# Cross attention: values stationary in four column tiles with turned probabilities moving, transposed output evicted and turned back, projections reordered

## The reference, cut to what matters

```python
q = _split_heads(query @ Wq + bq, B, S)
k = _split_heads(key @ Wk + bk, B, key.shape[1])
v = _split_heads(value @ Wv + bv, B, value.shape[1])
scores = jnp.einsum('bhqd,bhkd->bhqk', q, k) / jnp.sqrt(jnp.asarray(D_K, q.dtype))
p_attn = jax.nn.softmax(scores, axis=-1)
x = jnp.einsum('bhqk,bhkd->bhqd', p_attn, v)
x = x.transpose(0, 2, 1, 3).reshape(B, S, H * D_K)
return x @ Wo + bo
...
x = _layernorm(x + _L0_xattn_ref(x, ctx_1024, ctx_1024, ...), axis=-1)
```

## Time and profile before

| what | us |
|---|---|
| median of three executions | 1355.9 |
| the profiled execution | 1359.26 |
| its span in the profile | 1357.5 |
| cross attention, first `make_whole` to the last stored row | 358 to 636 |

### The profile page before, as it was taken

One profiled execution on the slowest core, in us unless ns is written; L12 is line 12 of the kernel. 1 busy time (PEld: TensorE's weight loads), 2 busy tenths in 40 slices (PEclk: granted clock), 3 DMA queues, 4 the chain that ended last, 5 costly groups with the idle time before them and its releaser, 6 DMA issues.

```text
span 1357.5 us, 25935 instructions
## 1 busy us (share of the span) xinstructions
PE 1031.1 (76%) x7366; PEld 774.2 (57%) x7367; DVE 1040.2 (77%) x2363; ACT 767.6 (57%) x1882; POOL 646.2 (48%) x869
## 2 busy tenths in 40 slices
PE   0236786654688888886788888885599999999980
PEld 0234343333566666664466666663588888888870
DVE  6893999997788888873788888873577777777765
ACT  4784643440688888883355555552166666666650
POOL 3895887774355555552244454442423232333324
PEclk9566888877688888886799999997699999999995
DMA  5944000003133333322012222222011111111105
GB/s 192 365 186 194 4 0 31 15 15 117 36 106 105 105 105 105 105 71 62 31 42 82 81 81 81 81 74 75 19 32 38 39 35 39 39 39 39 35 27 188
DMA packets 51884, 105.70 MB, mean 78 GB/s; under 512 B 9808, under 2 KB 36432, under 8 KB 51328
## 3 DMA queue, kind: packets, MB, share of 16 engines
q1 hardware_dynamic: 47472, 92.39, 19.7%
q0 software_dynamic: 4368, 12.78, 3.0%
HBM read 73.06 MB, written 32.10 MB: 77 GB/s over the span
## 4 chain that ended last, share of the span: by engine, by line
PE 35%; DVE 23%; ACT 13%; issue 11%; POOL 8%; DMA 2%; DVEq 0%; POOLq 0%; ACTq 0%; SPq 0%
PE banks L1965 14%; PE banks L1975 10%; POOL whole_level L1104 5%; ACT whole_level L1026 4%; DVE mix_sums L648 3%; ACT att_probs L1464 3%; PE banks L1363 2%; DVE carry L638 2%; DVE carry L635 2%; ACT whole_t L1042 1%; DVE kvq L1635 1%; PE banks L1376 1%; ACT whole L1035 1%; PE banks L1332 1%; DVE q_sin L1602 1%
## 5 line engine op out<-in xcount | busy, mean ns | idle before, releaser
L2048 DVE SCALAR_TENSOR_TENSOR expert_gate<-banks,expert_steps,expert_chunk 128x128 f32<-128x128 f32 x546 | 166.2, 346 | 96.6 <-ACT expert_chunk L2010 94.7
L1965 PE MATMUL banks<-expert_parts,levels 128*128 128x128 bf16 x3276 | 229.2, 220 | 8.1 <-issue 5.5
L1965 PEld LDWEIGHTS banks<-expert_parts,levels 128*128 x3276 | 203.0, 99 | 48.9 <-issue 21.2
L1975 PE MATMUL banks<-down,up 128*128 x546 | 176.2, 406 | 0.0
L2010 ACT COPY expert_chunk<-banks 128x256 f32<-128x256 f32 x273 | 101.7, 373 | 103.6 <-PE banks L1965 103.6
L2103 POOL DMA_INDIRECT chosen_d<-expert_y,expert_target x39 | 38.9, 998 | 204.0 <-ACT expert_y L2020 204.0
L1104 POOL TENSOR_SCALAR whole_level<-whole_level,whole_stat 128x128 f32<-128x128 f32 x112 | 89.3, 808 | 87.6 <-ACT whole_level L1026 87.6
L496 PE MATMUL banks<-x_turned,w_rkv 128*128 128x512 f32 (+1 forms) x192 | 100.5, 683 | 39.0 <-DVE weight L629 38.3
L2014 ACT ACTIVATE silu<-expert_gate,expert_steps 128x128 f32<-128x128 f32 x273 | 110.6, 405 | 15.9 <-DVE expert_gate L2048 15.7
L391 PE MATMUL banks<-consts,level 128*128 128x128 f32 x154 | 35.5, 423 | 87.3 <-POOL level L374 87.3
L2055 DVE SCALAR_TENSOR_TENSOR up<-expert_gate,expert_steps,silu 128x128 f32<-128x128 f32 x273 | 94.6, 346 | 9.3 <-ACT silu L2014 9.3
(11 more groups left out here) (240 smaller groups left out, 2597.6 us busy)
## 6 DMA issues: line engine op xcount, KB each, us to landing
whole_raw<-in_weight_jobs SPq DMA_DIRECT2D x16, 896.0 KB, 5.0
raw<-in_weight_jobs SPq DMA_DIRECT2D x11, 896.0 KB, 5.4
numbers_d<-turned SPq DMA_DIRECT2D x11, 896.0 KB, 5.0
levels_d<-whole_t SPq DMA_DIRECT2D x16, 448.0 KB, 2.7
levels<-levels_d SPq DMA_DIRECT2D x16, 448.0 KB, 3.6
down<-numbers_d SPq DMA_DIRECT2D x16, 448.0 KB, 4.4
finish_moe<-chosen_d SPq DMA_DIRECT2D x8, 512.0 KB, 7.6
normed_d<-normed_parts SPq DMA_DIRECT2D x16, 192.0 KB, 1.9
```

What stands on the lines that cost most here:

```text
L1965: last = pe.matmul(banks[:, at, (m * DC + c) * ROWS:(m * DC + c + 1) * ROWS], levels[:, bass.ds(expert * (2 * JOB) + (m * JOB + (f * DC + ...
L1975: last = pe.matmul(banks[:, Y + j, 0:D], up[j][:, f, :], down[:, bass.ds(expert * JOB + f * D, D)], start=(f == 0), stop=(f == FC - 1))
L2048: last = dve.scalar_tensor_tensor(out=gate[slot(j, f)][:, m, :], in0=halves(at)[:, m, 1, :], scalar=steps[j][:, m, 1, f:f + 1], in1=chunk[ ...
```

## The change: what it does

`sums` exchanges its operands. `v_ones` of a head, widened from 17 to 32 columns (16 values, a one, 15 zeros), is now stationary, and `probs_t` of the head moves, 128 columns. The output of a head is transposed (32 rows by 128 queries); four heads stand below each other in four column tiles (partitions 0, 32, 64, 96), in the second half of bank V. ACT copies the 128x256 of a half to `outs` (`take_outs`), PE turns it back with two 128x128 transposes (`turn_outs`) into HEADS, now 32 columns a head, and DVE's `normalise` reads it there.

The orders change with it. `front` gives up the v projection, which becomes `front_v`, called after `turn_heads`. On PE the output projection `join` goes from before `front` to behind `turn_outs(0, n)`, ahead of scores(0, n+1). On ACT `back` goes from the head of the step to behind `take_qk`. On DVE `normalise(n)` at the end becomes `normalise(n-1)` behind `peaks(1, n)`, and `join(n-1)` goes from before `take_values` to behind `steps_of`. SP and POOL are as before.

The new orders of one step n:

- PE: scores(1, n), turn_outs(1, n-1), turn_probs(0, n), front(n+1), turn_heads(n-1), front_v(n+1), tiles(0), sums(0, n), tiles(1), turn_probs(1, n), turn_outs(0, n), join(n-1), scores(0, n+1), tiles(2), sums(1, n), tiles(3).
- ACT: take_outs(1, n-1), collect(0, n), soften(1, n), take_x(n+1), make_whole(n), round_part 0, take_qk(n+1), back(n-1), tiles(0), round_part 1, take_outs(0, n), tiles(1), collect(1, n), tiles(2), round_part 2, tiles(3), soften(0, n+1).
- DVE: clip(n), peaks(1, n), normalise(n-1), take_values(n+1), steps_of(n+2), join(n-1), peaks(0, n+1).

```diff
 XH, XK = 16, 16
 HALF, QUAD = 8, 4
 BAND = QUAD * XK
+WIDE = 32
 QH, KVH, HD = 8, 2, 128
 REP = QH // KVH
 E, FFN = 8, 896
...
         q_t = [k.buffer(own, f"q_t{j}", [DC, S]) for j in range(2)]
         k_t = [k.buffer(own, f"k_t{j}", [DC, S]) for j in range(2)]
         spread = [k.buffer(own, f"spread{h}", [QUAD, S]) for h in range(2)]
-        v_ones = [k.buffer(own, f"v_ones{j}", [XH, XK + 1]) for j in range(2)]
+        v_ones = [k.buffer(own, f"v_ones{j}", [XH, WIDE]) for j in range(2)]
         x_bias = [k.buffer(own, f"x_bias{j}", [D]) for j in range(2)]
         peak = [k.buffer(own, f"peak{h}", [HALF]) for h in range(2)]
         probs = [k.buffer(own, f"probs{h}", [HALF, S]) for h in range(2)]
         probs_t = [k.buffer(own, f"probs_t{h}", [HALF, S]) for h in range(2)]
+        outs = [k.buffer(own, f"outs{h}", [2, S]) for h in range(2)]
         total = k.buffer(own, "total", [XH])
         heads = [k.buffer(own, f"heads{j}", [XH, XK]) for j in range(2)]
         heads_t = [k.buffer(own, f"heads_t{j}", [DC, S]) for j in range(2)]
...
     exp_ready = k.semaphore("exp_ready")
     probs_turned = k.semaphore("probs_turned")
     probs_t_ready = k.semaphore("probs_t_ready")
+    outs_summed = k.semaphore("outs_summed")
+    outs_ready = k.semaphore("outs_ready")
     heads_summed = k.semaphore("heads_summed")
     heads_ready = k.semaphore("heads_ready")
     heads_turned = k.semaphore("heads_turned")
...
         def front(j, n, i, begin=False):
 
             pe.wait_ge(rows_in[j], 32 * i + 32)
-            if not begin:
-                pe.wait_ge(heads_t_ready, n)
+            if not (isinstance(n, int) and n < 2):
+                pe.wait_ge(whole_read, ROUNDS * (n - 1))
             for c in range(DC):
                 last = pe.transpose(banks[:, TURN, c * P:(c + 1) * P], x_in[j][:, c * P:(c + 1) * P], k.ident)
             last.then_inc(x_turned, 1)
...
                     last = pe.matmul(banks[:, QK, m * P:(m + 1) * P], wq[:, c, m * P:(m + 1) * P],
                                      x_t[j][:, c, :], start=(c == 0), stop=(c == DC - 1))
             last.then_inc(qk_ready, 1)
-            if not begin:
+
+        def front_v(j, n):
+            if not (isinstance(n, int) and n == 0):
                 pe.wait_ge(v_read, n)
-                pe.wait_ge(joined_read, n)
+                pe.wait_ge(outs_ready, 2 * n - 1)
+            if not (isinstance(n, int) and n < 2):
+                pe.wait_ge(joined_read, n - 1)
             for c in range(DC):
                 last = pe.matmul(banks[:, V, 0:D], ctx_t[j][:, c, :], wv[:, c, :], start=(c == 0), stop=(c == DC - 1))
             last.then_inc(v_ready, 1)
...
                     last = pe.transpose(banks[:, PROBS_T + m, a * P:(a + 1) * P], probs[h][:, 4 * m + a, :], k.ident)
                 last.then_inc(probs_turned, 1)
 
-        def sums(j, h, n):
+        def sums(j, h, n, more):
 
             if h == 0:
-                pe.wait_ge(v_read, n + 1)
-                pe.wait_ge(heads_ready, n + 1)
+                pe.wait_ge(v_read, n + 1 + more)
+            else:
+                pe.wait_ge(joined_read, n + 1)
+            pe.wait_ge(outs_ready, 2 * n + h + 1)
             for m in range(2):
                 pe.wait_ge(probs_t_ready, 4 * n + 2 * h + m + 3)
                 for a in range(4):
                     head = HALF * h + 4 * m + a
-                    last = pe.matmul(banks[:, HEADS, head * (XK + 1):(head + 1) * (XK + 1)], probs_t[h][:, 4 * m + a, :],
-                                     v_ones[j][:, head, :], start=True, stop=True)
+                    last = pe.matmul(banks[WIDE * a:WIDE * (a + 1), V, D + m * S:D + (m + 1) * S], v_ones[j][:, head, :],
+                                     probs_t[h][:, 4 * m + a, :], start=True, stop=True)
+            last.then_inc(outs_summed, 1)
+
+        def turn_outs(h, n):
+
+            if h == 0:
+                pe.wait_ge(heads_ready, n + 1)
+            pe.wait_ge(outs_ready, 2 * n + h + 2)
+            for m in range(2):
+                last = pe.transpose(banks[:, HEADS, (2 * h + m) * P:(2 * h + m + 1) * P], outs[h][:, m, :], k.ident)
             if h:
                 last.then_inc(heads_summed, 1)
 
         def turn_heads(j, n, more):
             pe.wait_ge(heads_ready, n + 2)
-            pe.wait_ge(x_t_ready, n + 1 + more)
+            pe.wait_ge(x_t_ready, n + 2 + more)
             pe.wait_ge(whole_read, ROUNDS * n + ROUNDS)
             for c in range(DC):
                 last = pe.transpose(banks[:, TURN, c * P:(c + 1) * P],
                                     heads[j][:, HALF * c:HALF * (c + 1), :].rearrange("p h d -> p (h d)"), k.ident)
             last.then_inc(heads_turned, 1)
 
-        def join(j, n, more):
+        def join(j, n, taken):
 
             pe.wait_ge(heads_t_ready, n + 2)
-            pe.wait_ge(v_read, n + 1 + more)
+            pe.wait_ge(outs_ready, taken)
             for c in range(DC):
                 last = pe.matmul(banks[:, V, 0:D], heads_t[j][:, c, :], wo[:, c, :], start=(c == 0), stop=(c == DC - 1))
             last.then_inc(joined_ready, 1)
...
 
             scores(j, 1, n)
             if prev:
-                turn_heads(1 - j, n - 1, 1)
+                turn_outs(1, n - 1)
             turn_probs(0, n)
+            if more:
+                front(1 - j, n + 1, i + 1)
             if prev:
-                join(1 - j, n - 1, 1)
-            if more:
-                front(1 - j, n + 1, i + 1)
+                turn_heads(1 - j, n - 1, min(more, 1))
+            if more:
+                front_v(1 - j, n + 1)
             tiles(0)
-            sums(j, 0, n)
+            sums(j, 0, n, min(more, 1))
             tiles(1)
             turn_probs(1, n)
+            turn_outs(0, n)
+            if prev:
+                join(1 - j, n - 1, 2 * n + 2)
             if more:
                 scores(1 - j, 0, n + 1)
             tiles(2)
-            sums(j, 1, n)
+            sums(j, 1, n, 0)
             tiles(3)
 
         front(0, 0, 0, True)
+        front_v(0, 0)
         scores(0, 0, 0, True)
         in_steps(step, pe)
-        turn_heads(1, B - 1, 0)
-        join(1, B - 1, 0)
+        turn_outs(1, B - 1)
+        turn_heads(1, B - 1, -1)
+        join(1, B - 1, 2 * B + 1)
 
     def scalar(act):
         act.wait_ge(k.begun, k.begins["cross"])
         act.wait_ge(k.cross_loads, 16 * LOADS)
         act.sem_inc(heads_t_ready, 1)
         act.sem_inc(probs_t_ready, 2)
+        act.sem_inc(outs_ready, 1)
 
         def take_x(j, n):
             act.wait_ge(x_turned, n + 1)
...
                 act.copy(probs_t[h][:, 4 * m:4 * m + 4, :], banks[:, PROBS_T + m, :].rearrange(
                     "p (a s) -> p a s", a=4)).then_inc(probs_t_ready, 1)
 
+        def take_outs(h, n):
+            act.wait_ge(outs_summed, 2 * n + h + 1)
+            act.copy(outs[h][:, :, :], banks[:, V, D:2 * D].rearrange("p (m s) -> p m s", m=2)).then_inc(outs_ready, 1)
+
         def back(j, n):
             act.wait_ge(heads_turned, n + 1)
             act.copy(heads_t[j][:, :, :], banks[:, TURN, 0:D].rearrange("p (c s) -> p c s", c=DC)).then_inc(
...
                 take_whole(j, n, r, i + 1 - j if prev else 0)
 
             if prev:
-                back(1 - j, n - 1)
+                take_outs(1, n - 1)
             collect(0, n)
             soften(1, n)
             if more:
...
             if more:
                 round_part(1 - j, n + 1, 0)
                 take_qk(1 - j, n + 1)
+            if prev:
+                back(1 - j, n - 1)
             tiles(0)
             if more:
                 round_part(1 - j, n + 1, 1)
+            take_outs(0, n)
             tiles(1)
             collect(1, n)
             tiles(2)
...
             round_part(0, 0, part)
         soften(0, 0)
         in_steps(step, act)
+        take_outs(1, B - 1)
         back(1, B - 1)
 
     def gpsimd(pool):
...
 
         def normalise(j, n):
             dve.wait_ge(heads_summed, n + 1)
-            all_heads = banks[:, HEADS, 0:XH * (XK + 1)].rearrange("p (h d) -> p h d", h=XH)
+            all_heads = banks[:, HEADS, :].rearrange("p (h d) -> p h d", h=XH)
             st.did(dve.reciprocal(total[:, :], all_heads[:, :, XK]))
             st.wait()
             dve.tensor_tensor(heads[j][:, :, :], all_heads[:, :, 0:XK], wide(total[:, :], XK), ALU.mult).then_inc(
...
             clip(j, n)
             peaks(1, n)
             if prev:
-                join(1 - j, n - 1, i)
+                normalise(1 - j, n - 1)
             if more:
                 take_values(1 - j, n + 1)
             if more == 2:
                 steps_of(j, n + 2, i + 2 - j)
+            if prev:
+                join(1 - j, n - 1, i)
             if more:
                 peaks(0, n + 1)
-            normalise(j, n)
 
         dve.wait_ge(k.begun, k.begins["cross"])
         dve.wait_ge(k.cross_loads, 16 * LOADS)
...
         dve.sem_inc(heads_ready, 1)
         for j in range(2):
```

(15 more changed lines are left out.)

## The result

The changed kernel takes 1453.93 us (median of 4 executions, 1452.7 to 1455.59) against 1356.12 of the kernel before: ratio 1.0724, 95% interval 1.07 to 1.0749. It is slower by 98 us; 1466 were forecast, in a range of 1435 to 1500. Its profiled execution took 1455.08 us, 95.8 over that of before.

A forecast was written before the change was run, and what follows sets the result against it. A loop of DVE, ACT and PE was taken to close each 16.97 us step. 14 x (24.9 - 16.97) = +111.0, with -0.8 for the ends, gave 1469.5 profiled, 1466 us for the median; range 1435 to 1500.

The forecast's parts named there:

- T0: The end of DVE's second subtraction (L1138), the zero point of a step's times; one step lasted 16.97 us before.
- J: Start of DVE's join after T0: forecast +10.3 us, waiting for PE, or 12.3 with q and v also at the lower clock.
- T0': T0 one step on: 23.2 us at the full clock, 24.25 with scores and tiles at the lower, 24.9 taken.
- part 5: POOL's scale, bias and key spreading queue behind the join, so scores of half 0 start at J + 3.8 = 14.1 us.
- part 3: ACT's back precedes tiles(0), and take_outs(0) follows rounding part 1; PE then turns and joins, ready at +10.3 us.
- One sign: An expected trace sign: POOL's cross_ln waits for DVE some 5 us a step.
- the middle: Step length taken as 24.9 us, between PE's join at the full clock (24.25) and at the lower (25.5).
- The ends: Step 0, its clip about 2.3 us earlier, and the tail, +1.5 us; together -0.8.
- The sums: Matmuls of a half with exchanged operands on PE: 0.8 us taken, beside the loop, booked as 0 at the full clock.
- Rival 3: Column tiles don't run apart, at the lower clock: sums(1) delay the second scores, 1483 to 1510 us; 12%.
- Rival 4: Not slower: DVE's idle 2.2 us a step takes the join in; step 17.1 us, 1357 us in all; 5%.
- the chain of rows 4: Chain of waits for 484 to 500 us before the change: POOL's clip 34.6%, ACT's rounding 31.7%.

The follow-up runs named there:

- POOL's order turned: The changed kernel with POOL spreading the next sequence's keys before scale and add_bias: 1401.12 us, ratio 1.0315, a step of 20.48 us.
- the early copy: The changed kernel with POOL spreading keys before scale and add_bias, plus ACT's take_outs(0) right behind tiles(0), ahead of rounding part 1: 1389.75 us, ratio 1.0247.
- the filler: Four unused float32 matmuls of 512 columns put on PE between the join and scores(0) of the changed kernel: 1443.92 us, ratio 1.0647.
- v first: The kernel before with the v projection ahead of the wait for x_t and the q projection: 1357.88 us, ratio 1.0004.
- the version with the exchange, v first and 8 tiles: The old order with the operand exchange, v projection ahead of q, and DVE clipping 8 tiles in place of 7: 1358.08 us, ratio 0.9995.

## Why the prediction was right

- **The loop.** Foreseen and found, from T0: `take_values` +3.75 / +3.69; the join +10.3 / +10.48; scores(0) +14.1 / +14.32; their duration 2.08 / 2.08; ACT's tiles(2) copy at J + 5.45 + 1.05 = +16.8 / +16.98; the clip +19.8 / +19.91; T0' 24.25 / 24.32. POOL's place behind the join (part 5) was shown by taking it away: -4.0 us a step. The wait for `take_outs(0)` (part 3) likewise: -0.66. One sign was misjudged: POOL waits 10.60 us for the join's variance, where I wrote some 5; my own times, the clip's end at +1.2 and `scale` at +11.8, already gave 10.6. The sum doesn't use it.
- **The sum in parts.** Of the 7.5 us that a step lost, POOL's order holds 4.0 and the copy's place 0.7 (both measured, one after the other; the clock's share is in them, since the scores then start without PE's long wait). The other 2.85, from 19.82 to 16.97, is what is left with the join between the statistics and the peaks on DVE (from its row to the next peaks it is 2.8 us with POOL's order turned, 507.78 to 510.59, and with the early copy, 503.58 to 506.39), where before it lay in DVE's wait for v, which is now idle (3.06 us ahead of `take_values`). That share is argued from the timelines; the join was not moved back alone, since PE's join would have had to move with it.
- **The join's clock.** I took the middle of a join at the full and at the lower clock, 24.9. Twelve steps had the first, 24.3 (24.25 foreseen), and two the second: the join of the step from 522.18 ran at the lower level, DVE began it 11.56 after T0 (11.6 foreseen), and the step took 25.41 (25.5). The middle was a mean over two cases that hardly mix: of the 14.4 us by which the sum was too high for the profiled execution (110.2 against 95.8) it holds 14 x 0.42 = 5.9.

```profile
530.33 1.91 PE L959 MATMUL banks<-w_o,heads_t 128*128 128x256 f32 x4
532.28 0.42 DVE L1186 TENSOR_TENSOR joined<-banks,x_bias 128x256 f32<-128x256 f32 x1 [1.86 <-PE banks L959]
...
536.12 2.08 PE L907 MATMUL banks<-spread,q_t 64*128 64x512 f32 x4 [3.88 <-POOL spread L1122]
```

- **The ends.** Foreseen together -0.8, found -6.2: another 5.4. The last 3 lie in the later stages. I had costed both at the lower clock, as before. In the new kernel the clock was back early: in step 0 the turns took 1.09 at 363.74 and the scores behind them 1.13 where the earlier trace rows had 2.08, and the two joins of the tail took 1.22 and 1.13 where I booked 2.08 each. That is 1.8 of the tail's 3.9; the rest of it, and the 3 us of the later stages, stay unexplained.
- **The sums.** 0.64 us a half at the full clock, below the 0.8 I took, and up to 1.08 at the lower; 0 in the sum, as booked. Column tiles do run abreast: 16 passes of 128 columns in 0.64 us are 0.04 each, against 0.145 for the q projection's, and 0.11 for 128 columns of the filler's long passes (3.60 us for 8 of 512 columns, with one weight load each). That is 2.8 to 3.6 times, with four tiles. The estimate by the Trainium skill ("TensorE: Matmul & The Clock Gate", Part 3, measured speedup), which has 2.38 times for three tiles, was 1.0 us; the trace has less, with one tile more. Rival 3 is out.
- **Rival 4** (the step is set by the chain of rows 4) fell with the result, but the runs on the kernel before show that my reading of one closing loop was too sharp. Three loops, of ACT and POOL, of DVE, and of ACT, DVE and exp, seem to lie within half a microsecond of each other, with PE a fourth when its clock is low. That is read from the timelines; no run takes one loop away and leaves the clock as it was.

## What to carry to other kernels

When an instruction moves later on its engine, walk every in-order queue that waits for it and list what stands behind the wait there, not only the waiter: here a scalar power on POOL, at work a third of the time, held keys that needed nothing from it, and those held PE, ACT and the clip. Cost a matmul that a wait precedes at both clocks, and book the likelier one rather than the mean. Where three engines are each busy 85% of a step, several loops close at about the same length, and taking 11% of one engine's busy time away (138.66 to 123.63 us) moved the whole time by a tenth of a per cent.

## What the runs showed of the hardware

Keeping PE busy with useless matmuls made the changed kernel 0.7% faster. In the step of the first timeline the lower level (0.50) begins twice. First at about 510.6, 3.8 us after PE's join had ended, with PE idle in between; the rows are windows of half a microsecond, as in the earlier trace rows:

```profile
510.00:510.50 0.50, 0.00 (x0) 0.00 (x0) 0.00 (x0) 0.00 (x0) 0.50 (x1) 1.00 0.00 0
510.50:511.00 0.50, 0.28 (x2) 0.28 (x4) 0.00 (x0) 0.00 (x0) 0.50 (x2) 0.61 0.35 125
511.00:511.50 0.50, 0.50 (x2) 0.23 (x4) 0.00 (x0) 0.00 (x0) 0.50 (x1) 0.50 0.41 137
...
517.00:517.50 0.50, 0.00 (x0) 0.00 (x0) 0.50 (x3) 0.50 (x2) 0.50 (x2) 0.93 0.00 0
```

The idle time itself was granted 1.00; the price falls on the scores that end it. The second time is at about 517.4, when PE had been idle for only 0.8 us behind the second scores (515.48, 1.13 us). PE's busy time and its clock also went opposite ways between two versions: from 400 to 560 us, v first had PE busy 149.03 us at a mean clock of 0.80, and the version with the exchange, v first and 8 tiles had it busy 115.23 at 0.97. A part of the first figure is the lower clock's own doing, since the same matmuls last longer at it (the turns above 1.91 in place of 1.04 us), and these runs do not separate the two.
